# First pass of a cross-attention kernel: the score matmuls that feed the row maximum, moved to 32-row tiles

## The reference

```python
qh = (q @ Wq.T + bq).reshape(B, Sq, N_HEAD, D_HEAD)
kh = (k @ Wk.T + bk).reshape(B, Sk, N_HEAD, D_HEAD)
vh = (v @ Wv.T + bv).reshape(B, Sk, N_HEAD, D_HEAD)
scores = jnp.einsum('bqhd,bkhd->bhqk', qh, kh) / np.sqrt(D_HEAD)
scores = jnp.where(attention_mask[:, None, :, :], NEG_FILL, scores)
probs = jax.nn.softmax(scores, axis=-1)
out = jnp.einsum('bhqk,bkhd->bqhd', probs, vh)
```

## Time and profile before

| | |
|---|---|
| device time, median of 3 runs (lowest, highest) | 548.28 (548.16, 549.21) |
| the profiled execution: its time | 549.37 |
| its span, first to last instruction | 547.7 |
| mean granted TensorE clock | 0.959 of full |
| busy: PE, PE weight loads | 506.7 (93%), 439.5 (80%) |
| busy: ACT, DVE, POOL | 380.0 (69%), 299.4 (55%), 101.6 (19%) |
| load of a context block, issue to landing, median | 6.9 |
| store of a key half, high and low, median | 7.0 and 7.1 |

### The profile page before, as it was taken

One profiled execution on the slowest core, in us unless ns is written; L12 is line 12 of the kernel. 1 busy time (PEld: TensorE's weight loads), 2 busy tenths in 40 slices (PEclk: granted clock), 3 DMA queues, 4 the chain that ended last, 5 costly groups with the idle time before them and its releaser, 6 DMA issues.

```text
span 547.7 us, 14225 instructions
## 1 busy us (share of the span) xinstructions
PE 506.7 (93%) x5620; PEld 439.5 (80%) x5620; DVE 299.4 (55%) x432; ACT 380.0 (69%) x377; POOL 101.6 (19%) x101
## 2 busy tenths in 40 slices
PE   6799999999999999999549999999999999969987
PEld 3699988988889888989438988998899889848544
DVE  5757988988889888989948910000000000036465
ACT  3258777777777777777539999999999999923111
POOL 5583322233123321330500000000000000000000
PEclk8889999999999999999959999999999999979699
DMA  8554577455865577595793787777777777000000
GB/s 292 174 237 115 210 275 278 168 187 234 289 214 172 201 280 272 164 409 224 273 403 93 281 289 274 269 282 277 280 285 289 289 289 290 4 2 1 1 0 10
DMA packets 34759, 117.45 MB, mean 214 GB/s; under 512 B 4401, under 2 KB 10417, under 8 KB 34737
## 3 DMA queue, kind: packets, MB, share of 16 engines
q1 hardware_dynamic: 30560, 110.58, 54.5%
q0 software_dynamic: 4032, 6.42, 4.4%
q10 hardware_dynamic: 144, 0.13, 0.1%
HBM read 74.44 MB, written 39.47 MB: 208 GB/s over the span
## 4 chain that ended last, share of the span: by engine, by line
PE 55%; DMA 14%; issue 9%; POOL 8%; DVE 8%; ACT 5%; SPq 0%; POOLq 0%; ACTq 0%; DVEq 0%
PE ps_a L945 19%; PE ps_k L959 17%; DMA early<-in_ctx 13%; POOL k_stack L340 8%; PE ps_k L811 4%; PE ps_a L853 4%; PE ps_a L820 3%; ACT k_stack L396 3%; PE ps_a L862 2%; DMA v_in<-in_wv 1%; PE ps_a L1052 1%; PE ps_a L888 1%; PE ps_a L1090 1%; DVE early L655 1%; DVE block_max L627 1%
## 5 line engine op out<-in xcount | busy, mean ns | idle before, releaser
L627 DVE TENSOR_REDUCE block_max<-ps_a 128x1 f32<-128x896 f32 x112 | 121.5, 1085 | 12.3 <-PE ps_a L853 9.8
L945 PE MATMUL ps_a<-q_stack,k_stack 128*128 128x256 f32 x784 | 111.3, 294 | 1.8 <-ACT middle L485 1.0
L853 PE MATMUL ps_a<-k_hi,q_pad 128*128 128x448 f32 x448 | 110.5, 368 | 2.6 <-DVE block_max L627 2.6
L945 PEld LDWEIGHTS ps_a<-q_stack,k_stack 128*128 128x128 f32 x784 | 99.5, 191 | 14.2 <-issue 11.4
L432 ACT CAST early<-ps_a 128x896 bf16<-128x896 f32 x104 | 94.3, 907 | 23.6 <-PE ps_a L853 23.4
L485 ACT ACTIVATE middle<-ps_a 128x1536 f32<-128x1536 f32 (+1 forms) x56 | 90.3, 1662 | 12.9 <-PE ps_a L945 12.8
L485 ACT ACTIVATE early<-ps_a 128x1536 f32<-128x1536 f32 (+1 forms) x56 | 90.2, 1662 | 7.8 <-PE ps_a L945 7.8
L688 DVE COPY early<-ps_k 128x512 f32<-128x512 f32 x1 | 0.7, 691 | 170.6 <-PE ps_a L999 170.6
L853 PEld LDWEIGHTS ps_a<-k_hi,q_pad 128*128 128x128 f32 x448 | 79.7, 189 | 10.6 <-DVE block_max L627 4.1
L340 POOL TENSOR_TENSOR k_stack<-early,k_stack 128x448 fp32r<-128x448 f32 x52 | 59.6, 1150 | 146.2 <-DVE early L622 119.7
L811 PE MATMUL ps_k<-k_stack,w_hi 128*128 128x448 f32 x224 | 58.8, 385 | 12.8 <-DVE k_lo L580 8.7
(11 more groups left out here) (174 smaller groups left out, 437.4 us busy)
## 6 DMA issues: line engine op xcount, KB each, us to landing
k_stack<-k_hi_scratch SPq DMA_DIRECT2D x56, 448.0 KB, 6.1
v_scratch<-early SPq DMA_DIRECT2D x14, 952.0 KB, 8.2
v_in<-v_scratch SPq DMA_DIRECT2D x14, 952.0 KB, 7.8
early<-in_ctx SPq DMA_DIRECT2D x14, 896.0 KB, 6.9
k_hi_scratch<-k_hi SPq DMA_DIRECT2D x28, 448.0 KB, 7.0
k_lo_scratch<-k_lo SPq DMA_DIRECT2D x28, 448.0 KB, 7.1
k_stack<-k_lo_scratch SPq DMA_DIRECT2D x28, 448.0 KB, 6.3
mask_b<-in_maskn POOLq DMA_DIRECT2D x14, 224.0 KB, 6.9
```

Source lines behind the costliest of these rows:

```text
L627: nc.vector.tensor_reduce(block_max[:, par, taken:taken + 1], ps_a[:, 2 * BUFFER[par][h]:2 * BUFFER[par][h] + 2, 0:HK], AX.XY, ALU.max).th ...
L853: last = nc.tensor.matmul(out, q_pad[:, h, :], k_hi[:, par, m, n * HK:(n + 1) * HK], start=True, stop=not masked)
L945: last = nc.tensor.matmul(ps_a[:, bank, (k % 2) * 2 * Q:(k % 2 + 1) * 2 * Q], k_stack[:, b_par, a, t * P:(t + 1) * P], q_stack[:, a, :, :] ...
```

## The change

Only the first pass and the reduction behind it. A group u (0 to 7 of a block) replaces a pair of heads: four heads by half a block. The four heads lie on the four 32-row quarters of the partitions, and the matmul of each reads only the 32 rows of its quarter (q_pad and k_hi), each writing to a bank of its own. The number of matmuls (32 per step, 448 columns each) and of copied and reduced elements is the same. Each group gives two banks to ACT and two to DVE. ACT's pair is always banks 0 and 1; DVE's alternates between 2, 3 and 4, 5. So before group u PE waits for ACT's copy of group u-1 and for DVE's reduction of group u-2. DVE reduces along the last axis into two columns and takes the running maximum for two heads of half a block; running rows are now 448 long for all 16 heads. Only even slots are left, eight per step, LAG is four groups. DVE does the slot's low keys ahead of its maxima. From step 2 on ACT copies the context's high part in four pieces, one after the score copy of each of the first four slots, and POOL's pieces follow them one by one, still gated by DVE's maxima in the same four slots. SP issues the load of a context block behind the stores of the block's first key half rather than ahead of them. At the end one tree over 16 rows of 448 replaces three trees over 2, 4 and 2 rows of 896, plus one small maximum. (Cut; `load`, `store_keys` and `store_values` are the old code in pieces.)

```diff
-VIA_ACT = (1, 3, 5, 7, 9, 11, 13, 15)
-NA = len(VIA_ACT)
-ND = H - NA
+TILE_ROWS = P // 4
+NG = H // 2
 PIECES = 4
-PIECE_AFTER = (9, 11, 13, 15)
-BUFFER = [[(par * H + h) % 3 for h in range(H)] for par in range(2)]
 
...
+        def group_heads(u):
+            m, e, n = u // 4, u // 2 % 2, u % 2
+            rows = ((2, 3), (0, 1)) if n == 0 else ((0, 1), (2, 3))
+            return [[(j, m * HT + 2 * j + e) for j in part] for part in rows]
+
+        def copied_rows(u):
+            return running[:, 2 * (u ^ 1):2 * (u ^ 1) + 2, :]
+
+        def pair_scores(u, w):
+            bank = w * (2 + 2 * (u % 2))
+            return ps_a[:, bank:bank + 2, 0:HK]
+
         def scored_in(slot):
-
-            return (1, slot + LAG) if slot < H - LAG else (0, slot - (H - LAG))
-
-        def running(h):
-            k = VIA_ACT.index(h)
-            return run_early[:, k, :] if k < 2 else run_middle[:, k - 2, :] if k < 6 else run_late[:, k - 6, :]
+            u = slot // 2
+            return (1, u + LAG) if u < LAG else (0, u - LAG)
 
...
             with sp.Fori(1, NB // 2) as i:
-                load(i * 2, 0)
-                store(i * 2 - 2, 0)
-                load(i * 2 + 1, 1)
-                store(i * 2 - 1, 1)
+                for par in range(2):
+                    s = i * 2 - 2 + par
+                    store_keys(s, par, 0)
+                    load(s + 2)
+                    store_keys(s, par, 1)
+                    store_values(s, par)
 
...
-                pool.wait_ge(ctx_hi_ready, s + 1)
                 for n in range(PIECES):
+                    pool.wait_ge(ctx_hi_ready, s * PIECES + n + 1)
                     if not first:
-                        pool.wait_ge(run_taken, (s - 2) * NA + VIA_ACT.index(PIECE_AFTER[n]) + 1)
+                        pool.wait_ge(run_taken, (s - 2) * NG + LAG + n + 1)
...
+            def high_piece(s, par, n):
+                c, half = n // 2, slice(n % 2 * HK, (n % 2 + 1) * HK)
+                act.wait_ge(ctx_in, s * 16 + 16)
+                nc.scalar.copy(ctx_hi[:, par, c, half], ctx_t[:, c * BK:(c + 1) * BK][:, half]).then_inc(ctx_hi_ready, 1)
 
...
+            def copy_scores(s, u):
+                act.wait_ge(max_scored, s * NG + u + 1)
                 if isinstance(s, int) and s == 0:
-                    nc.scalar.copy(running(h).rearrange("p (n k) -> p n k", n=2), scores).then_inc(run_taken, 1)
+                    nc.scalar.copy(copied_rows(u), pair_scores(u, 0)).then_inc(run_taken, 1)
                 else:
-                    act.wait_ge(run_taken, s * NA + k - 1)
-                    nc.scalar.copy(staged[:, (par * NA + k) % 2, :].rearrange("p (n k) -> p n k", n=2),
-                                   scores).then_inc(max_copied, 1)
+                    act.wait_ge(run_taken, s * NG + u - 1)
+                    nc.scalar.copy(staged[:, u % 2], pair_scores(u, 0)).then_inc(max_copied, 1)
 
             def evacuate(s, par, first, last=False):
-                def prepare():
-
-                    if not first:
-                        act.wait_ge(max_scored, (s - 1) * H)
-                    if not last:
-                        if not (first and par == 0):
-                            act.wait_ge(v_projected, s * NV)
-                        high_context(s + 1, 1 - par)
-
                 if not first:
-                    prepare()
+                    act.wait_ge(max_scored, (s - 1) * NG)
                     act.wait_ge(v_stored[par], (s - par) * 8)
                 for slot, work in enumerate(PROJECTIONS):
                     if first and slot == PREPARE_SLOTS[par]:
-                        prepare()
-                    if work and work[0] == "v":
+                        if par == 1:
+                            act.wait_ge(v_projected, s * NV)
+                        high_context(s + 1, 1 - par)
+                    if slot % 2:
+                        continue
+                    if work[0] == "v":
                         evacuate_values(s, par, work[1])
-                    if work and work[0] == "k":
+                    else:
                         evacuate_keys(s, par, work[1], work[2], first)
-                    of_last, h = scored_in(slot)
-                    if h in VIA_ACT and not (of_last and first and par == 0):
-                        copy_scores(s - of_last, (1 - par) if of_last else par, h)
+                    of_last, u = scored_in(slot)
+                    if not (of_last and first and par == 0):
+                        copy_scores(s - of_last, u)
+                    if not first and not last and slot < 2 * PIECES:
+                        if slot == 0:
+                            act.wait_ge(v_projected, s * NV)
+                        high_piece(s + 1, 1 - par, slot // 2)
 
...
+            def maximum(s, par, u):
+                dve.wait_ge(max_scored, s * NG + u + 1)
+                nc.vector.tensor_reduce(block_max[:, par, 2 * u:2 * u + 2], pair_scores(u, 1), AX.X, ALU.max).then_inc(max_taken, 1)
+                if not (isinstance(s, int) and s == 0):
+                    dve.wait_ge(max_copied, (s - 1) * NG + u + 1)
+                    nc.vector.tensor_tensor(copied_rows(u), copied_rows(u), staged[:, u % 2], ALU.max).then_inc(run_taken, 1)
+                if u == NG - 1:
+                    dve.wait_ge(max_taken, s * NG + NG)
+                    nc.vector.tensor_tensor(row_max[:], row_max[:], block_max[:, par, :], ALU.max).then_inc(row_max_ready, 1)
                     dve.wait_ge(row_max_ready, s + 1)
-                    dve.wait_ge(run_taken, s * NA + NA)
-
-            def step(s, par, slots=range(H)):
+                    dve.wait_ge(run_taken, s * NG + NG)
+
+            def step(s, par, slots=range(0, H, 2)):
                 for slot in slots:
                     work = PROJECTIONS[slot]
-                    of_last, h = scored_in(slot)
-                    maximum(s - of_last, (1 - par) if of_last else par, h)
-                    if work and work[0] == "k":
+                    if work[0] == "k":
                         low_keys(s, par, work[1], work[2])
-
-            step(0, 0, range(H - LAG, H))
+                    of_last, u = scored_in(slot)
+                    maximum(s - of_last, (1 - par) if of_last else par, u)
+
+            step(0, 0, range(H - 2 * LAG, H, 2))
             step(1, 1)
             with dve.Fori(1, NB // 2) as i:
                 step(i * 2, 0)
                 step(i * 2 + 1, 1)
-            for h in range(LAG, H):
-                maximum(NB - 1, 1, h)
-
-            for tiles, at in ((run_early, ND), (run_middle, ND + 2), (run_late[:, :, :], ND + 6)):
-                width = BK // 2
-                while width >= BK // 8:
-                    link(nc.vector.tensor_tensor(tiles[:, :, 0:width], tiles[:, :, 0:width], tiles[:, :, width:2 * width],
-                                                 ALU.max))
-                    width //= 2
-                link(nc.vector.tensor_reduce(row_max[:, at:at + tiles.shape[1]], tiles[:, :, 0:2 * width], AX.X, ALU.max))
+            for u in range(LAG, NG):
+                maximum(NB - 1, 1, u)
+
+            width = HK // 2
+            while width >= HK // 8:
+                link(nc.vector.tensor_tensor(running[:, :, 0:width], running[:, :, 0:width], running[:, :, width:2 * width],
+                                             ALU.max))
+                width //= 2
+            link(nc.vector.tensor_reduce(run_max[:], running[:, :, 0:2 * width], AX.X, ALU.max))
+            link(nc.vector.tensor_tensor(row_max[:], row_max[:], run_max[:], ALU.max))
 
...
+            def score_for_max(s, par, u, masked):
+                m, n = u // 4, u % 2
+                if u % LAG == 0:
                     pe.wait_ge(hi_ready, (s * DC + m + 1) * 2)
-                if h == 0 and masked:
+                if u == 0 and masked:
                     pe.wait_ge(mask_in[par], (s - par) * 8 + 16)
-                pair = BUFFER[par][h]
-                earlier = [a for a in range(h) if BUFFER[par][a] == pair]
-                before = earlier[-1] if earlier else max(a for a in range(H) if BUFFER[1 - par][a] == pair)
-                back = 0 if earlier else 1
-                if not (isinstance(s, int) and s == 0 and back):
-                    if before in VIA_ACT and isinstance(s, int) and s - back == 0:
-                        pe.wait_ge(run_taken, VIA_ACT.index(before) + 1)
-                    elif before in VIA_ACT:
-                        pe.wait_ge(max_copied, (s - back - 1) * NA + VIA_ACT.index(before) + 1)
-                    else:
-                        rank = before - sum(a < before for a in VIA_ACT)
-                        pe.wait_ge(max_taken, (s - back) * ND + rank + 1)
-                for n in range(2):
-                    out = ps_a[:, 2 * pair + n, 0:HK]
-                    last = nc.tensor.matmul(out, q_pad[:, h, :], k_hi[:, par, m, n * HK:(n + 1) * HK],
```

(22 more changed lines are left out.)

86 lines of the change are left out of this document (31 added, 55 removed).

## The result

The changed kernel takes 524.19 (median of 4 runs, 522.12 to 524.74) against 548.22 (547.95 to 549.21): ratio 0.9542, 95% interval 0.9519 to 0.9564. Its profiled execution took 524.74, with a span of 523.0. The prediction was 525.5 with a range of 512 to 542, so the total is right. The parts of the sum are less so, and the experiments say more than the total does.

The account below looks back on a forecast made before the run. PE bound the kernel, DVE 6 to 12% behind; eleven steps 18.2, steps 1 and last 1.1, step 0 0.5, drain 1.4, tree 1.4 total 22.6 saved from 549.4 or median 548.3; predicted 525.5, range 512 to 542.

Parts of the forecast that it names:

- PE's price of a group: First-pass scores: four 32-row tile matmuls plus both mode switches take PE 0.60, bringing its step from 16.4 to 14.65.
- rival B: Scores: wide weight loads go one by one, a group costs 0.91, PE's step 17.1 stays the bound; 541, chance 0.13.
- rival D: Scores: row tiles don't run side by side and pay both switches, 1.16 a group, step 19.1; 569, chance 0.11.
- rival A: Scores: clean overlap without switch cost, 0.28 a group, DVE bounds; 517, or 513 with a faster restart; chance 0.15.
- DVE as the next bound: First-pass steps: DVE's work does not shrink and takes PE's place as bound, 15.0 per step against PE's 14.65.
- PE's hand-over: PE waiting for ACT's copy of the fixed bank pair: 0.4 per step added to 15.5, making 15.9.
- The drain: Four groups after the last projection, bound by copy and score on the fixed pair: 7.5 instead of 8.9, -1.4.
- sign 6: In the changed profile, drain plus tree take about 12.6 in place of 15.4.
- Low keys first: DVE's low keys ahead of maxima: key bank freed 1.5 earlier, cost nothing; could help PE's k_lo wait, 3.5 in four steps.
- SP's order: Context load moved behind two key stores: lands 16.3 after a step's start, wanted at 17.4, slack 1.1.
- Rival C: Context ring stays the bound: load lands 1.5 later or pieces trail the last maximum, step about 16.7; 536, chance 0.11.
- The stall: Steps of the kernel before: 1.1 per step beyond matmul time, going once ACT's 1.7 context copy leaves the path.

Follow-up runs that it names:

- one-quarter kernel: The changed kernel with all four matmuls of a group reading the same 32 rows (0 to 31), giving wrong scores; 602.92, ratio 1.1003.
- uneven pieces: The changed kernel with each context half cut at column 352 instead of 448, making POOL's piece behind a key slot's maximum shorter; 520.62, ratio 0.9485.
- short-reduction kernel: The changed kernel with DVE's reduction reading only the first 224 of 448 columns of each bank; 518.62, ratio 0.9473.
- the zeros: The changed kernel with context halves cut at column 352, plus PE matmuls of zeros into an idle bank through drain and tree; 516.35, ratio 0.9405.
- the quarters alone: The kernel before with only ACT's context copy split into four pieces after its first four score copies, POOL's pieces following; 545.72, ratio 0.9976.

## Why the prediction was right, and where it was not

**PE's price of a group: right, in both halves.** I took 0.60, from 0.28 for four tiles side by side and 0.34 for both switches. Measured: 0.60, of it 0.21 for the tiles and 0.39 for the switches. The other ends fell with it: loads are not one behind another (rival B), the rows do run side by side (rival D, whose 1.16 the one-quarter kernel nearly shows: 1.00 + 0.19), and the switches are not free (rival A). On A, by the Trainium skill (TensorE: Matmul & The Clock Gate, Measured speedup vs the span model), 3.07 times for four row tiles would have meant 0.27 a group, an estimate from that page. The traces do not agree with it: 0.21 for the tiles alone is 3.9 times, and 0.60 with the switches 1.4 times. The Trainium skill (TensorEngine Tiling, Key Properties) says that a change of tiling mode drains the engine; the trace agrees in kind, with 0.39 of the 0.60, and that decided.

**DVE as the next bound: right, but not carried through.** I had 15.0, and 0.3 for POOL's overlap only under rival A. Measured 15.33: the two maxima that run beside POOL are 0.19 longer each, which is the difference. A row of before pointed at it: DVE's 61.85 over four steps is 15.46 a step, not 15.0. The uneven pieces took back 0.24 of it, down to where PE is the bound. I then took 15.9 because I added PE's hand-over to the longer of the two engines in each pair of slots. That step failed: 15.5 + 0.4 should have been PE's own sum plus the hand-over, 14.65 + 0.4 = 15.05 (15.09 in the short-reduction kernel), beside DVE's 15.3, the larger of the two counting over the whole step. As I read it, with DVE's two bank pairs PE can run ahead in one pair of slots and be caught up in the next, so the longer engine of each pair does not add up. The eleven steps came 11 x 0.57 = 6.2 shorter than forecast. That the missing 0.4 is the hand-over was not shown by itself.

**The drain: wrong.** I took it as bound by copy and score on the fixed pair, 7.5 for four groups, and 1.4 shorter than before. Counting the last step as 15.33, it runs from 237.58 to the tree at 246.53: 8.95, and no gain. DVE's timeline of the changed kernel there:

```profile
238.66 1.08 DVE L626 TENSOR_REDUCE block_max<-ps_a 128x2 f32<-128x896 f32 x1
239.66 0.62 DVE L629 TENSOR_TENSOR early<-early 128x896 bf16<-128x896 bf16 x1
240.20 1.08 DVE L626 TENSOR_REDUCE block_max<-ps_a 128x2 f32<-128x896 f32 x1
...
244.80 1.08 DVE L626 TENSOR_REDUCE block_max<-ps_a 128x2 f32<-128x896 f32 x1
```

DVE has no gap: it enters the drain a group behind PE, and five groups at 1.53 apiece and the small maximum are 7.9 from 238.66 on. PE's half clock (0.50 from 240, its group 0.75) cost nothing there, since the drain with the zeros is as long. The tree fell by 1.3 as forecast, so drain and tree together take 14.1 and not the 12.6 of sign 6. The last step, 0.5 shorter than forecast, hides part of this in the table's 0.9. The 1.5 either way for the phase of the clock's restart has no row behind it.

**What made up for the steps.** 0.9 in the last step and drain, and code that the change doesn't touch: +0.9 ahead of the first key projection and +1.7 in the wait before PE's first instruction after the weighted sums. Across the executions of this study that wait is 2.5 to 2.7 in some and 3.0 to 4.3 in others, for kernels with the same code there, and the first key projection starts between 27.1 and 28.5. So the agreement to 1.3 is in good part luck: between the profiled executions the steps gave 6.6 more than forecast (6.2, and 0.4 in step 1), and everything else 4.5 less.

**Low keys first: wrong.** "Cost nothing, covered by DVE being the bound; uncovered it could only help the 3.5 wait." It is worth 22 in the changed kernel and costs 18 in the old grouping. The prediction checked who waits for k_lo and not what is queued behind a DVE that stands for ACT.

**SP's order: wrong in kind.** I asked whether the moved load would still be in time, and gave 1.1 of slack. The question was whom the load had been holding back: the store of the low keys, and through the single k_lo area DVE. The earlier trace rows did not show it, since the wait lay just under another. Rival C looked at the load's landing, which fell from 6.9 to 5.6. The prediction gave the moved load no price at all; added to the quarters it is worth 12.

**The stall.** That 1.1 per step was no matmul time held: 16.49 without it. That the quarters alone would remove it was wrong (1.3 of 11.5).

Priced by the ratios along a path on which no part loses: quarters 1, load behind the stores 12, tiles with their grouping, banks and order 12; together 25.

## What to carry to other kernels

A wait that ends last hides others just under it: before pricing its removal, follow each queue and each single buffer round its own loop, since here a store behind a waiting load took the place of the stall at once. The price of a part found by undoing it in a balanced kernel is no price of its gain, since waits pile up and the clock may fall behind them. Add parts in order from the other side too, and expect the sign of an order (low keys first) to depend on which engine runs ahead. Four row tiles took the time of one matmul here, and a visit to them and back 0.39 on top, so group them: eight tile matmuls in one visit cost 0.81 (0.62 + 0.19), in two visits 1.20. And in a drain ask which engine comes into it with work left over.

## What the runs showed of the hardware

- Four 448-column matmuls on four 32-row quarters take PE 0.21 together; on one quarter some 0.8. Their 128-column weight loads lie within 0.19 for all four. Full array to row tiles and back costs 0.39, and nothing in the same groups on the full array.
- A PE that is busy without a pause is not granted the full clock in every case: 24.2 at 0.50 with all tiles of a group on one quarter, where the same number of tiles on four quarters ran at 1.00. Why was not tried.
- A bf16 maximum on DVE over 896 elements takes 0.61 to 0.62, and 0.80 when a POOL subtraction overlaps its start; low keys, which read PSUM (0.67 at 167.52), did not lengthen beside POOL.
- The granted clock fell to half in the drain: PE was busy 1.63 of the 4 us from 236 to 240, and the clock is 0.50 from 240 on. It stayed at 1.00 when matmuls of zeros filled the drain and the tree behind; 4.3 less in the medians, 1.8 in the traces.
- Landing times follow bunching: with the stores spread, a key half's store lands in 3.7 against 7.0, a context load in 5.6 against 6.9. With the load first again in the changed kernel they are 7.0 and 6.6.
